# A pipeline of eight layers on one core: four streams in place of three, and LoRA's maxima by pairs of heads

## The reference

```python
x = x + geo_attention(ln(x))      # 8 heads of 16, causal, a rank-one term per head added to the scores
x = x + moe0(ln(x))               # 8 experts, 512 hidden, one expert a token by argmax, sigmoid gate
x = x + diff_block(ln(x))         # per token, 32 x 32 scores between heads; softmax, difference, rms; then FF 512
x = x + mx_linear(ln(x))          # fp6 block quantisation of input and weight, one product
x = x + lora_attention(ln(x))     # 16 heads of 8, not causal
x = x + moe2(ln(x))               # 14 experts, 256 hidden, gelu, softmax gate
x = x + wide_attention(ln(x))     # 16 heads with 128-wide queries and keys, values of 8, causal
x = x + moe3(ln(x))               # 8 experts, 128 hidden, capacity 512 with positions counted over all tokens
```

## Time and profile before

| | us |
|---|---|
| median of 3 runs | 3041.17 |
| lowest, highest | 3022.04, 3044.92 |
| the profiled execution | 3002.18 |
| its span, first to last instruction | 3001.0 |
| TensorE busy | 2090.2 (70%) |
| VectorE busy | 1728.2 (58%) |
| ScalarE busy | 1143.4 (38%) |
| GpSimd busy | 665.1 (22%) |
| DMA engines busy, hardware queue | 22.1% |

### The profile page before, as it was taken

One profiled execution on the slowest core, in us unless ns is written; L12 is line 12 of the kernel. 1 busy time (PEld: TensorE's weight loads), 2 busy tenths in 40 slices (PEclk: granted clock), 3 DMA queues, 4 the chain that ended last, 5 costly groups with the idle time before them and its releaser, 6 DMA issues. The chain is left out here.

```text
span 3001.0 us, 42829 instructions
## 1 busy us (share of the span) xinstructions
PE 2090.2 (70%) x13457; PEld 1445.4 (48%) x13457; DVE 1728.2 (58%) x4326; ACT 1143.4 (38%) x2744; POOL 665.1 (22%) x904
## 2 busy tenths in 40 slices
PE   4530775689856895589847895689858895578483
PEld 3330542456443653457444654457445654354352
DVE  2346548565765668465765667465856667453132
ACT  0320432355433553245323553245324552254251
POOL 2015013401251014300250014200250024200101
PEclk9775875699667996789678986789678976897695
DMA  6120141203040313213140313212140503211402
GB/s 179 43 71 0 22 118 36 80 20 116 25 137 15 96 43 92 82 32 104 30 140 7 113 37 95 67 57 80 38 134 1 129 29 90 59 22 33 139 1 59
DMA packets 263737, 200.32 MB, mean 67 GB/s; under 512 B 28708, under 2 KB 236964, under 8 KB 262980
## 3 DMA queue, kind: packets, MB, share of 16 engines
q1 hardware_dynamic: 257348, 184.77, 22.1%
q0 software_dynamic: 6144, 12.60, 1.4%
HBM read 151.18 MB, written 35.49 MB: 62 GB/s over the span
## 5 line engine op out<-in xcount | busy, mean ns | idle before, releaser
L1230 ACT ACTIVATE mid_room<-ps 128x512 f32<-128x512 f32 x256 | 153.1, 598 | 171.9 <-PE ps L940 171.6
L1184 ACT ACTIVATE late_room<-ps 128x384 f32<-128x384 f32 x256 | 125.7, 491 | 210.1 <-PE ps L865 206.7
L1196 ACT ACTIVATE late_room<-ps,late_neg_max 128x128 f32<-128x128 f32 (+1 forms) x512 | 186.7, 420 | 22.2 <-DVE late_neg_max L1566 19.3
L1031 PE MATMUL ps<-mid_pool 128*128 128x128 f32 x544 | 122.4, 361 | 91.2 <-DMA mid_pool<-moe_small 64.9
L1589 DVE TENSOR_REDUCE mid_room<-ps 128x2 f32<-128x512 f32 x256 | 163.8, 686 | 37.2 <-PE ps L927 34.5
L1565 DVE TENSOR_REDUCE late_neg_max<-ps 128x1 f32<-128x128 f32 x256 | 73.9, 289 | 188.8 <-PE ps L857 188.7
L938 PE MATMUL ps<-mid_pool 48*128 48x256 bf16 x512 | 164.9, 322 | 21.1 <-DVE max_rows L1604 20.3
L940 PE MATMUL ps<-max_rows,of_unit 96*128 96x256 bf16 x512 | 166.9, 326 | 0.0
L855 PE MATMUL ps<-late_aT,heads_T 128*128 128x256 f32 x512 | 162.5, 401 | 0.0
L1743 DVE TENSOR_TENSOR early_pool<-ps,early_pool 128x1024 f32<-128x1024 f32 x128 | 150.7, 1219 | 15.5 <-ACT early_pool L1286 11.2
L1268 ACT ACTIVATE mid_room<-ps,mid_pool 128x128 f32<-128x128 f32 x272 | 85.2, 364 | 183.9 <-PE ps L1031 183.4
(11 more groups left out here) (379 smaller groups left out, 5361.0 us busy)
## 6 DMA issues: line engine op xcount, KB each, us to landing
mid_pool<-in_m_w_dram SPq DMA_DIRECT2D x272, 128.0 KB, 2.1
early_pool<-m_folded_w SPq DMA_DIRECT2D x88, 256.0 KB, 3.2
early_pool<-in_m_w_dram SPq DMA_DIRECT2D x88, 256.0 KB, 3.1
mid_pool<-mid_room SPq DMA_DIRECT2D x192, 64.0 KB
heads_T<-in_m_w_dram SPq DMA_DIRECT2D x176, 64.0 KB, 1.9
mid_pool<-moe_small SPq DMA_DIRECT2D x136, 65.0 KB, 2.0
mid_room<-moe_sorted_in SPq DMA_DIRECT2D x32, 256.0 KB, 3.0
moe_sorted_out<-mid_room SPq DMA_DIRECT2D x32, 256.0 KB, 2.4
```

The source lines that it names most:

```text
L1031: mm = pe.matmul(ps[:, B + b % h_banks, c * P:(c + 1) * P], table[:, c * P:(c + 1) * P], rows_T[s][:, b, :], start=True, stop=True)
L1196: ins = act.activation(probs[s][:, n % RING, qt, 0:w], ps[:, bank, qt * P:qt * P + w], ACT.Exp, bias=neg_max[s][:, n % RING, qt:qt + 1])
L1230: act.activation(probs_T[s][:, n % (2 * QUAD), :], ps[:, B + slots.index(("unit", n)) % S_BANKS, :], ACT.Exp)\
```

## The change

1. **Four streams.** EARLY keeps geo and moe0 and has banks 0 and 1. The new SECOND has bank 2 alone and does differential attention, its feed-forward part and MX. MID keeps LoRA and moe2, LATE is as before. The blocks become E, ES, ESM, five ESML in the loop, SML, ML and L. New order strings are written for each.
2. **Rings.** `S_BANKS` gives way to the stream's banks without the last for causal attention, so one for geo and two for wide, and to both banks for LoRA. moe0's first layer has one bank.
3. **Differential attention.** ScalarE copies q, k and v (384 columns) of each tile to a ring of three in SBUF; VectorE reads them there, and TensorE waits for the copy only. VectorE's product of a quarter is followed at once by its reduction, with a wait between. The four feed-forward products share one bank.
4. **Geo** keeps queries and keys unpadded and contracts 17 rows of one strip. GpSimd's clearing of the queries is gone. Values are stored densely, 17 or 9 columns a head.
5. **Tables.** Each expert's whole table lies in one row of DRAM and is fetched by one DMA; three tables in SBUF in place of four. MOE0's rows are written in the preparation; ScalarE's queue copies those of moe2 and moe3 once the weights are loaded, and the second block waits for them.
6. **x** is loaded into EARLY's own tile when a block begins, not a block ahead into a spare tile.
7. **LoRA's maxima** are made for two heads at a time, their matmuls taking turns.

```diff
-TABLES = 4
-TABLE_DMAS = 3
+TABLES = 3
+    def score_banks(self, at):
+        return self.banks if at is LORA else self.banks - 1
-EARLY = Stream("early", 0, 3, ["geo_in", "geo_out", "moe0_router", "diff_in", "diff_out"],
-               ["v", "o", "conn"])
-MID = Stream("mid", 3, 2, ["diff_ff", "mx_in", "lora_in", "lora_out", "moe2_in"], ["ff", "mx", "v", "o"])
+EARLY = Stream("early", 0, 2, ["geo_in", "geo_out", "moe0_router"], ["v", "o"])
+SECOND = Stream("second", 2, 1, ["diff_in", "diff_out", "diff_ff", "mx_in"], ["conn", "ff", "mx"])
+MID = Stream("mid", 3, 2, ["lora_in", "lora_out", "moe2_in"], ["v", "o"])
...
+            @block.scalar
+                act.wait_ge(weights_here, LOADED)
+                for dst, src in later_copies:
+                        act.dma_start(dst, src).then_inc(later_tables, 16)
...
-                    sp.dma_start(tables[s][:, i, 0:m.w2_at], layer1[m][:, bass.ds(expert, 1), :]).then_inc(here, 16)
-                    sp.dma_start(tables[s][:, i, m.w2_at:m.b2_at],
-                                 layer2[m][:, bass.ds(expert * m.chunks, m.chunks), :]).then_inc(here, 16)
-                    sp.dma_start(tables[s][:, i, m.b2_at:m.width],
-                                 small[m][bass.ds(expert * P, P), :]).then_inc(here, 16)
+                    sp.dma_start(tables[s][:, i, :].unsqueeze(1), whole[m][:, bass.ds(expert, 1), :]).then_inc(here, 16)
...
                     k = slots.index((kind, n))
-                    if k >= S_BANKS:
-                        before_kind, before_n = slots[k - S_BANKS]
+                    ring = s.score_banks(at)
+                    if k >= ring:
+                        before_kind, before_n = slots[k - ring]
...
-                        if n >= S_BANKS:
-                            pe.wait_ge(sig("max_ready"), n - S_BANKS + 1)
+                    def maxima_scores(pair):
+                        for n in pair:
+                            if n >= s.banks:
+                                pe.wait_ge(sig("max_ready"), n - s.banks + 1)
                         for qt in range(SEQ_TILES):
+                            for n in pair:
...
-                        geo_v[:, :], lambda h: geo_q[:, h, :],
-                        lambda h: geo_k[:, h // 4, :], "geo_out", geo_wo[:, :])
+                        geo_v[:, :], lambda h: geo_q[geo_rows(h), h // 4, :],
+                        lambda h: geo_k[geo_rows(h), h // 4, :], "geo_out", geo_wo[:, :])
...
-                        if t >= 2:
-                            pe.wait_ge(qkv_used, t - 1)
-                        pe.matmul(ps[:, B + t % 2, 0:3 * DIM], aT[s][:, t * P:(t + 1) * P], diff_w[:, :],
+                        if t >= 1:
+                            pe.wait_ge(qkv_kept, t)
+                        pe.matmul(ps[:, B, 0:3 * DIM], aT[s][:, t * P:(t + 1) * P], diff_w[:, :],
...
-                        if c >= 2:
-                            pe.wait_ge(dh_kept, c - 1)
+                        if c >= 1:
+                            pe.wait_ge(dh_kept, c)
...
+                if EARLY in streams:
+                    sp.dma_start(x[EARLY][:, :, :], load_from).then_inc(x_here, 16)
+                    sp.wait_ge(x_here, 16)
...
-            group_block(block, [EARLY], x_v[:, 1 * TILES:2 * TILES, :],
-                        None)
+            group_block(block, [EARLY], x_v[:, 0:TILES, :], None)
+        nc.sync.wait_ge(later_tables, 16 * len(later_copies))
         next_turn()
         with nc.Block(no_gpsimd_drain=True) as block:
-            group_block(block, [EARLY, MID], x_v[:, 2 * TILES:3 * TILES, :],
-                        None)
+            group_block(block, [EARLY, SECOND], x_v[:, TILES:2 * TILES, :], None)
+        next_turn()
+        with nc.Block(no_gpsimd_drain=True) as block:
+            group_block(block, [EARLY, SECOND, MID], x_v[:, 2 * TILES:3 * TILES, :], None)
```

More of the change, by code:

```diff
@@ L288, in sequence_model @@
             rstd[s] = own("rstd", [P, 2, TILES])
-            v_pad[s] = own("v_pad", [P, TILES, heads, STRIP])
+        for s, at, m in ((EARLY, GEO, MOE0), (MID, LORA, MOE2), (LATE, WIDE, MOE3)):
+            own = lambda name, shape, dt=F32: sb(f"{s.name}_{name}", shape, dt)
+            v_pad[s] = own("v_pad", [P, TILES, at.heads * (at.v_depth + 1) + STRIP])
             inv_sum[s] = own("inv_sum", [P, 16, 1])
@@ L764, in early, with second @@
                     yield from experts(EARLY, MOE0)
-                    yield from steps(len(WEIGHTS[EARLY]) - len(causal_weights(EARLY, GEO))
-                                     - len(experts_weights(MOE0)))
+                def second():
+                    yield from steps(len(WEIGHTS[SECOND]))
                 def mid():
-                    yield from steps(len(FF_STEPS))
                     yield from steps(4)
@@ L1453, in late @@
                     yield from experts(LATE, MOE3, zz[LATE])
-                take_steps(streams, [early() if s is EARLY else mid() if s is MID else late() for s in streams])
+                programs = {EARLY: early, SECOND: second, MID: mid, LATE: late}
+                take_steps(streams, [programs[s]() for s in streams])
             @block.vector
```

402 lines of the change are left out of this document (196 added, 206 removed).

## The result

The changed kernel takes 3042.46 us (median of 20 runs, 3029.89 to 3055.94), the kernel before 3025.95 beside it (20 runs, 3007.43 to 3047.53): a ratio of 1.0046 [1.0028, 1.0063]. The forecast was 2816, a ratio of 0.926 to the 3041.17 that I then had. The two profiled executions took 3002.18 and 3049.96, further apart than the medians, so single blocks are compared to about 1%.

What follows compares the result with a forecast made beforehand. Full blocks were taken as bound by order, with TensorE at a lower clock beside VectorE's stage. 78 + 162 + 185 + 255 + 5 x 293 + 252 + 232 + 150 = 2779 us, scaled to 2816; range 2690 to 2970.

Steps and rivals of the forecast that it cites:

- smaller edits: Table fetches, three tables, memset, q copies and ScalarE's wider copies: zero for all of these together.
- the ring and the hidden bank in E: Block E, 162 us in all: one bank adds 21 for geo's scores, 5 for values, 4 for moe0's hidden layer.
- the 17 rows: Geo's scores between 128-row masks: no separate term; the full block's added 24 us hold it once, hidden in part.
- The wait for the ring: Geo in full blocks: steps 5 us apart exceed the 2.9 us chain, so exposure small outside E and ES.
- The overlap in the full block: ESML: half of 48 us of other TensorE work added to LoRA and moe2's chain; 293 taken, between 273.5 and 311.7.
- The drains: Geo's row-height changes cost 4.2 us a group, 34 us if exposed in all eight groups: 2850; chance 0.09.
- The slower rival: One-bank rings hold up every stream: 26 plus some 16 us a full block, 354; whole 3184 or 3225; chance 0.09.
- The "nothing" rival: The extra block and longer ramp lose the gain: full blocks of about 335 us, whole 3030; chance 0.05.
- The preparation: Before block E: 78 us, bounds 68 (copies covered) and 92 (folded table's write waits for most copies).
- ESM: Third block: the old EM's stages side by side instead of behind each other, 255 us, between 243 and 282.8.
- The signs: Right: full blocks 280 to 310 us, last-third clock near 0.9, E 150 to 175; wrong: preparation and ramp over 1400.
- The factor 1.013: Whole sum: profiled execution 3002.2 was 1.3% under the median 3041.2, so 2780 is scaled to 2816.

Runs made afterwards that it cites:

- a1: The changed kernel with geo's score products over all 128 rows (scores no longer geo's): 2989.76 us, 0.9851 of the kernel before.
- a9: The changed kernel with LATE's idle first bank as second bank for geo's ring and moe0's hidden layer in E, ES, ESM: 2990.26 us, 0.9874 of the kernel before.
- a8: The changed kernel with four tables again for moe2 and moe3, three for moe0: 2992.41 us, 0.9865 of the kernel before.
- a2: The changed kernel with ScalarE writing v's copy in reading order, by a second copy a tile: 3014.64 us, 0.9948 of the kernel before.
- c4: c3 with geo's score products over all 128 rows (scores no longer geo's): 2839.53 us, 0.9370 of the kernel before.
- b1: The kernel before with geo's score products over 17 rows, two banks in the ring as before: 3107.24 us, ratio 1.0259.
- b2: The kernel before with one bank for geo's scores and values and one for moe0's hidden layer: 3172.34 us, ratio 1.0444.
- c3: The changed kernel with a2, a8 and a9 together, and the table-row copies moved to SyncE's queue in block E: 2902.30 us, 0.9611 of the kernel before.

## Why the prediction was wrong

- **The step that failed** is the price of what the fourth stream is bought with: EARLY's slim form and the "smaller edits". I priced the ring and the hidden bank in E, as latency at full speed (21 + 5 + 4 us), the 17 rows at nothing in the sum and as drains in a rival, and tables and copies of q, k and v as "zero for all of these together". In the new plan itself the rows cost 1.9% (a1), the missing second bank in E, ES and ESM 1.7% (a9), the third table 1.8% (a8) and v's stride 1.0% (a2). Mended together, with the copies moved (c4), they are 203 us of the 226 between measured and forecast.
- **The mechanism that was missing** is the clock. The 17 rows lost it with TensorE busy 90% of the time (0.55 for 1.00), the ring of one by its gaps (0.56), and some 210 instructions that had taken 24 busy us took 47 (b1, 84 to 138) and 43 (b2). A cost in hand-overs or drains can be added up in advance; this one stood nowhere in the prediction.
- **The wait for the ring** was judged better than the two items above suggest. In the old order b2 adds 18.0 us to a full block, with 14.5 to 15.8 us of waits; in the new order, which the prediction spoke of ("5 us a step, more than the chain of 2.9"), 5.4 us of waits a block are left.
- **The overlap in the full block** was too hopeful as well. I let TensorE fill half of its idle time, from 80.8 us to 43; it came to 71.8. Rows, stride and tables mended bring the block to 306.2, but mostly by shorter busy time (237 us); its idle time is 70 still. (213 of 273.5 us is 78%, not 79; nothing hangs on it.) What holds those waits up was not found, nor was SECOND's single bank tested (its waits on ScalarE, L1110, are 1.6 us in the block above).
- **The drains** had the right price, 3.8 for 4.2 us a group. What the 17 rows did to the clock is more than the drains: b1 lost 81 us where the drains make 31.
- **The slower rival** named one-bank rings at 42 us a full block, as waits. In the old order b2 shows 18.0 for their part in EARLY. The "nothing" rival had the time (3030) with another cause: full blocks are 325, not 335, and the rest is in ESM, E and ES.
- **What the trace could have told.** L1031's 64.9 us of waiting for moe2's tables in the kernel before is a whole-run row, and I had read only one block's 6.8. The price of v's stride could not be read there, since v lay in PSUM.
- **The preparation** was 6 over, and about 4 in the nine other profiles with it: the folded table's landing did wait for the copies, between my middle and my upper bound (92).
- **ESM** was my most hopeful term, 255 between 243 and 282.8, and came out at 292.8, above the upper end, because that end took over the old block's clock (0.73), and the new one has 0.63.
- **The signs** that I had named were mixed. Preparation and ramp came to 1425 us, over the 1400 that was to show me wrong; the full blocks missed 280 to 310 and E just missed 175. The last third's clock, the missing wait on q, k and v, and the fetches 1.1 us apart came as forecast.

c4 takes 2839.53, 0.8% over the forecast of 2816, and that closeness is partly luck. E is 30 us under its term, thanks to the spare bank, and the five full blocks are 66 over theirs. The factor 1.013 came from a median of three; with the 3025.95 of twenty runs it is 1.008, and the forecast 2801. How much of the 13 us that c4's full block is over its term comes from the ring of one that it still has was not measured: all eight banks are in use, so a second one can't be given.

## What to carry to other kernels

When a change gives a stream fewer banks or smaller products, price the clock beside the wait: look whether the stretch now runs at the upper level, and cost the same instructions at the lower one too. To price a form that comes with a new plan, put the form alone into the old plan; that bounds the plan's worth, but waits that the old order exposes may be hidden in the new one, so take the parts back out of the new plan too. And undo suspects together as well as singly, since in a thin block two causes of a low clock each hide the other.

## What was unexpected of the hardware

- Products over 17 rows between 128-row masks left TensorE at 0.55 while 90% busy; the same over 128 rows had 1.00 at 76% (b1's and the old kernel's windows), and 0.57 against 0.92 in c3 and c4. From the same full clock, the stretch with 2.84 busy us in 4 lost it and the one with 2.27 kept it.
- In b2 the clock was 1.00 from 84 to 92 us, with no gap over 1.5 us, then fell, and was 0.50 from 92.5 to 150, where 1.20 us of each 3.63 us step were a gap.
- A VectorE product of 1024 elements a partition with a stride of eight floats took 2.04 us from SBUF and 1.22 from PSUM; in reading order 1.42 from SBUF.
- Eight copies in short runs on ScalarE's queue delayed a transfer on SyncE's queue by 11 to 14 us (81.7 to 84.34 against 70.42 for the step behind it), though its issue was not touched.
